# Six heads of an attention transpose by blocks and DMA instead of four, a rounding rest on another engine, and a new order of three roundings

## The chip, the cores and the metric

One core of a Trainium2 chip runs one program. The metric is the device time of that program in microseconds (us). The engines of the core are TensorE (PE in the profile, its weight loads PEld), VectorE (DVE), ScalarE (ACT), GpSimd (POOL) and SyncE (SP); each has its own stream of instructions and they meet at semaphores.

## The reference, cut to what matters

There are 128 graphs of 128 nodes with 512 features. Each graph goes through two layers.

```python
# --- layer 0: attention over the graph, 8 heads of 64 units
h = jnp.maximum(_layernorm(x), 0.0)
feats = jnp.einsum('bnf,hfu->bhnu', h, W)
dense = leaky_relu(e_self[..., :, None] + e_neigh[..., None, :], 0.2) + NEG_BIG * (1 - A)
att = softmax(dense, axis=-1)
x = x + relu(jnp.einsum('bhij,bhju->bhiu', att, feats) + b)      # heads side by side
# --- layer 1: hypergraph convolution twice, 512 -> 1024 -> 512
h = jnp.maximum(_layernorm(x), 0.0)
r = relu(Dn * H (Be * H^T (h @ W1^T)) + b1)                      # H = adj != 0
x = x + Dn * H (Be * H^T (layer_norm(r) @ W2^T)) + b2 + h        # y + x of the layer, then the residual
```

## The kernel before

The work runs in turns. In turn t the engines work on several graphs at once: the attention logits of graph t+3, the exponentials of graph t+2 (and the rest of those of t+1), the applying of the attention of t+1, the first large product (`hidden`, 512 to 1024) of graph t, the second large product (1024 to 512) of graph t-1 and the last small product of graph t-2. `turns` writes turns -5 to 1 out, loops over the middle with four turns in a loop body, and writes the last turns out. In every engine's `turn` the order of the instructions is written by hand; each engine works through its list in order, and `wait_ge` holds all that stands behind it.

The large products are made from fp32r parts: an operand is rounded by ScalarE ("hi"), the rest ("lo" = value - hi) is made by another engine, and TensorE adds hi*hi, hi*lo and lo*hi. So `hidden` needs `hg_hi` (ScalarE L572) for its first eight products and `hg_lo` (VectorE L844) for the four behind them (L890, function `low`). The second product needs `rT_hi` (ScalarE L579) and `rT_lo` (VectorE L652). The last product needs `z_hi` (ScalarE L565) and `z_lo` (GpSimd L407).

The attention weights must be transposed before they are applied. Heads 4 to 7 go through TensorE (L939), ScalarE copies them out of PSUM (L507), and they are applied at L959. Heads 0 to 3 are transposed in blocks of 32x32 by VectorE (L841, `attB`), written to HBM (L283, `att_blocks`) and read back by four DMAs (L293) that put the blocks where they belong; they are applied at L962 after a wait on `s_attD`. The exponentials come in two halves (`exps`), each head as two activations (L460, L461) whose larger one VectorE takes (`larger`, L628).

TensorE's list in one turn is: `hidden`, the last product, the four transposes, the features of chunks 0 and 1, the applying of eight heads, the second product, the features (2,0), `hg` (L992: h times G_rs, in plain fp32), the other features with the logits, and the counts p_G (L1011). VectorE's list from the end of the second product is: `z` (L792), the statistics of an x that a DMA brought (L798), the logits (L808, L818), an aggregate (L821), the transpose `eT` (L834), `attB` (L841), `hg_lo` (L844), and then the next turn's features and `rT_lo`. ScalarE's list there is: `h` (L556), `z_hi`, `hg_hi`, `rT_hi`, a copy of G. GpSimd's is: G_lo, `z_lo`, two small operations for a standard deviation (`rstd`), then a wait for the DMA that brings `u`. SP's list from eT on is: en_rows (L279), att_blocks (L283), u (L287), and the four attT transfers (L293).

Of the kernel before, what the change touches and what calls it, by code (L numbers as in the profile page):

```python
# [4 lines left out]
F32 = mybir.dt.float32  # L5
# [59 lines left out]
def gnn_two_layers(nc, x, xT, adj2, W0T, W0U, b0, a_diag, W1T, b1, gammaT, betaT, W2T, b2, out):  # L65
# [5 lines left out]
    HALF = 512  # L71
    HH = HEADS // 2
    CB = HC // 2
    UE = UN + 1
# [6 lines left out]
    with ctx:  # L81
# [55 lines left out]
        neg_max = sb("neg_max", [P, HEADS])  # L137
        attB = sb("attB", [P, HH * N])
        attT = sb("attT", [P, HEADS, N])
# [58 lines left out]

        att_blocks = nc.dram_tensor("att_blocks", [P, HH * N], F32, kind="Internal").ap()

# [28 lines left out]
        def _(sp):  # L229
# [40 lines left out]
            def turn(t):  # L270
# [18 lines left out]
                if t.plus(1).within(NG):  # L289

                    sp.wait_ge(s_attB_out, t.plus(1).count(per=16))
                    for c in range(4):
                        sp.dma_start(attT[32 * c:32 * (c + 1), 0:HH, :].rearrange("b k (q a) -> b k q a", q=4),  # L293
                                     att_blocks.rearrange("(q b) (k c a) -> c b k q a", q=4, c=4, a=32)[c]).then_inc(s_attD, 16)
# [31 lines left out]
        def _(pool):  # L326
# [19 lines left out]

            def turn(t):
                g = t.plus(2)
                if g.within(NG):
# [49 lines left out]
                if g.within(NG):  # L399
# [7 lines left out]
                    nc.gpsimd.tensor_tensor(z_lo[:, :], z[:, :], z_hi[:, :], ALU.subtract).then_inc(s_z_lo, 1)  # L407
                g = t.plus(5)
                if g.within(NG):
                    if g.has(1):  # L410
                        pool.wait_ge(s_rs0, g.count(1))
                    if g.has(4):
                        pool.wait_ge(s_feats_sb, g.count(4, per=2))
                        pool.wait_ge(s_es_low, g.count(4))
                    rstd(g, mv0, ve0, rs0[:, g.slot(4):g.slot(4) + 1], s_mv0, s_ve0, s_rs0)

# [3 lines left out]
        def _(act):  # L420
# [31 lines left out]

            def exps(g, half):

                act.wait_ge(s_shifts, g.count())
                if g.has(1):
                    act.wait_ge((s_attB, s_attT)[half], g.count(1))
                    act.wait_ge(s_att, g.count(1, per=2))
                for i in range(half * HH, (half + 1) * HH):
                    nc.scalar.activation(att[:, i, :], u[:, g.slot(2), i, :], ACT.Exp, bias=shifts[:, 0, i:i + 1])  # L460
                    last = nc.scalar.activation(att_low[:, i, :], u[:, g.slot(2), i, :], ACT.Exp, bias=shifts[:, 1, i:i + 1],  # L461
                                                scale=SLOPE)
                    if i == 2:
                        load_x(g.plus(3))
                last.then_inc(s_exp, 1)

            def turn(t):
                if t.plus(1).within(NG):

                    exps(t.plus(1), 1)  # L470
                g = t.plus(3)
# [30 lines left out]
                if g.within(NG):  # L502

                    act.wait_ge(s_attT, g.count())
                    if g.has(1):
                        act.wait_ge(s_o, g.count(1))
                    nc.scalar.activation(attT[:, HH:HEADS, :].rearrange("p h n -> p (h n)"), p_att[:, HALF:2 * HALF],  # L507
                                         ACT.Copy).then_inc(s_attT_sb, 1)
# [40 lines left out]
                if g.within(NG):  # L549

                    act.wait_ge(s_nm1, g.count())
                    if g.has(2):

                        act.wait_ge(s_hg, g.count(2))
                        act.wait_ge(s_xh, g.count(2))
                    nc.scalar.activation(h[:, g.slot(2), :], x1[:, g.slot(2), :], ACT.Relu, bias=nm1[:, :]).then_inc(s_h, 1)  # L556
                    if g.base == 0:
                        rounded(3)
                g = t.plus(-1)
                if g.within(NG):  # L560
# [4 lines left out]
                    nc.scalar.activation(z_hi[:, :], z[:, :], ACT.Copy).then_inc(s_z_hi, 1)  # L565
                g = t.plus(1)
                if g.within(NG):

                    act.wait_ge(s_hg, g.count())
                    if g.has(1):  # L570
                        act.wait_ge(s_w1, g.count(1, per=2))
                    nc.scalar.activation(hg_hi[:, :], p_w1b[:, :], ACT.Copy).then_inc(s_hg_hi, 1)  # L572
                g = t
# [26 lines left out]
        def _(dve):  # L600
# [22 lines left out]

            def larger(g, half):

                dve.wait_ge(s_exp, g.count(per=2) - 1 + half)
                heads = slice(half * HH, (half + 1) * HH)
                nc.vector.tensor_tensor(att[:, heads, :], att[:, heads, :], att_low[:, heads, :], ALU.max).then_inc(s_att, 1)  # L628
# [7 lines left out]
            def turn(t):  # L636
                g = t.plus(2)
                if g.within(NG):
# [8 lines left out]
                    feats_of(g, 1, scale)  # L647
                g = t.plus(-1)
                if g.within(NG):

                    dve.wait_ge(s_rT_hi, g.count())
                    nc.vector.tensor_tensor(rT_lo[:, :].rearrange("p (k q a) -> p k q a", q=4, a=32), rT_chunks,  # L652
                                            rT_hi[:, :].rearrange("p (k q a) -> p k q a", q=4, a=32), ALU.subtract).then_inc(s_rT_lo, 1)
                g = t
# [8 lines left out]
                if t.plus(1).within(NG):  # L663
                    larger(t.plus(1), 1)
                g = t.plus(3)
# [43 lines left out]
                if g.within(NG):  # L709
                    dve.wait_ge(s_r, g.count(per=2))  # L710
                    if g.has(1):
                        dve.wait_ge(s_rB_out, g.count(1, per=16))
                    if g.base == 0:
                        rest_of(3, k_lo2)
                        rest_of(4, k_lo2)
                        dve.wait_ge(k_lo2, 2)
                    nc.vector.transpose(rB, r[:, :]).then_inc(s_rB, 1)  # L717
# [5 lines left out]
                if g.within(NG):  # L723
# [9 lines left out]
                    if g.has(1):  # L733
                        dve.wait_ge(s_exp, g.count(1, per=2))
                    nc.vector.tensor_tensor(shifts[:, :, :], e_blk[:, SELF:SELF + EW].rearrange("p (a h) -> p a h", a=2),  # L735
# [86 lines left out]
                if m.within(NG + 2):  # L822
# [9 lines left out]
                    if g.has(2):  # L832
                        dve.wait_ge(s_exp, g.count(2, per=2))
                    nc.vector.transpose(eT[:, :], e_blk[:, :]).then_inc(s_eT, 1)  # L834
                g = t.plus(2)
                if g.within(NG):

                    dve.wait_ge(s_att, g.count(per=2) - 1)
                    if g.has(1):
                        dve.wait_ge(s_attB_out, g.count(1, per=16))  # L840
                    nc.vector.transpose(attB[:, :], att[:, 0:HH, :].rearrange("p h n -> p (h n)")).then_inc(s_attB, 1)  # L841
                if t.plus(1).within(NG):
# [6 lines left out]
        def _(pe):  # L849
# [59 lines left out]
            def transposes(dst, src, s):  # L909
                for c in range(HALF // P):  # L910
                    last = nc.tensor.transpose(dst[:, c * P:(c + 1) * P], src[:, c * P:(c + 1) * P], ident[:, :])
                last.then_inc(s, 1)

            def turn(t):
                g = t
# [17 lines left out]
                if g.within(NG):  # L933

                    pe.wait_ge(s_att, g.count(per=2))
                    if g.has(1):
                        pe.wait_ge(s_osc, g.count(1))
                    for i in range(HH, HEADS):
                        last = nc.tensor.transpose(p_att[:, i * N:(i + 1) * N], att[:, i, :], ident[:, :])  # L939
                    last.then_inc(s_attT, 1)  # L940
                g = t.plus(3)
                if g.within(NG):
# [7 lines left out]
                    for c in range(2):  # L950
                        features(c, 0)
                        features(c, 1)
                g = t.plus(1)
                if g.within(NG):

                    pe.wait_ge(s_attT_sb, g.count())
                    pe.wait_ge(s_feats_sb, g.count(per=2))
                    for i in range(HH, HEADS):
                        mm(p_o[:, i // HH, i % HH, :], attT[:, i, :], feats[:, g.slot(2), i, :], start=True, stop=True)  # L959
                    pe.wait_ge(s_attD, g.count(per=64))  # L960
                    for i in range(HH):
                        last = mm(p_o[:, 0, i, :], attT[:, i, :], feats[:, g.slot(2), i, :], start=True, stop=True)  # L962
                    last.then_inc(s_o, 1)
                if t.base == -1:
# [3 lines left out]
                if g.within(NG):  # L968

                    pe.wait_ge(s_rT_hi, g.count())  # L970
                    if t.within(NG):
                        pe.wait_ge(s_pre, t.count(per=2) - 1)
                    for c in range(HC):
                        if g.base == 0 and c % CB == 0:
                            pe.wait_ge(k_lo2, 1 + c // CB)
                        high(p_w1a[:, :], rT_hi[:, part(c)], W2_hi[:, c, :], W2_lo[:, c, :], c == 0)
                    pe.wait_ge(s_rT_lo, g.count())
                    for c in range(HC):
                        last = low(p_w1a[:, :], rT_lo[:, part(c)], W2_hi[:, c, :], c == HC - 1)
                    last.then_inc(s_w2, 1)  # L980
                g = t.plus(3)
                if g.within(NG):
                    features(2, 0)
                g = t.plus(1)
# [75 lines left out]
```

## Time and profile before

| | |
|---|---|
| median of 3 runs | 2440.66 us (2439.64 to 2444.9) |
| the profiled execution | 2446.31 us, of which the span of the trace is 2444.5 us |
| busy share of the span | PE 97%, PEld 84%, DVE 84%, ACT 70%, POOL 56% |
| HBM traffic | 166 GB/s over the span |

The span runs from the first to the last instruction. A busy TensorE need not be a fast one, since its instructions overlap; what counts is the step from one start to the next.

### The profile page before, as it was taken

The page shows a single profiled execution, that of the slowest core. Times are in us where ns is not written, and L with a number is a line of the kernel's source. Part 1 is how long each engine was busy: PE and PEld are TensorE (multiplying, and loading weights), DVE is VectorE, ACT ScalarE, POOL GpSimd, SP SyncE. Part 2 cuts the span into 40 slices and gives each one's busy share as a digit, 9 for nine tenths or more (in the row PEclk, how much of TensorE's full clock was granted, in tenths as well). Part 3 has the DMA queues.
Part 4 walks back from the last instruction along what each step waited for, and adds up shares of the span by engine and source line. Part 5 has one row for each costly group of instructions (what it writes and reads, how often), then busy time and mean ns, then how long its engine had stood idle before and what let it go on. Part 6 is the DMA issues. An engine that isn't in the chain of part 4 may idle for free.

```text
span 2444.5 us, 50002 instructions
## 1 busy us (share of the span) xinstructions
PE 2382.7 (97%) x13492; PEld 2049.6 (84%) x13492; DVE 2053.7 (84%) x4501; ACT 1713.1 (70%) x4489; POOL 1372.0 (56%) x1549
## 2 busy tenths in 40 slices
PE   5799999999999999999999999999999999999997
PEld 3688888888888888888888888888888888888886
DVE  3888888888888888888888888888888888888884
ACT  2577777777777777777777777777776777777774
POOL 2356556556556556556556556556555555555553
PEclk9799999999999999999999999999999999999999
DMA  6355555555555555555555555555555555555542
GB/s 218 104 167 170 166 171 170 167 170 169 168 171 169 167 170 170 167 170 171 168 169 169 167 170 169 167 170 170 168 169 164 172 164 170 171 167 171 172 145 86
DMA packets 494608, 405.34 MB, mean 166 GB/s; under 512 B 310648, under 2 KB 392568, under 8 KB 494584
## 3 DMA queue, kind: packets, MB, share of 16 engines
q1 hardware_dynamic: 474072, 367.30, 50.8%
q10 hardware_dynamic: 20512, 37.76, 5.5%
q8 instruction: 10, 0.16, 0.0%
q14 instruction: 14, 0.11, 0.0%
HBM read 268.58 MB, written 136.35 MB: 166 GB/s over the span
## 4 chain that ended last, share of the span: by engine, by line
PE 89%; DVE 4%; issue 2%; DMA 1%; ACT 1%; DVEq 0%; POOL 0%; POOLq 0%; ACTq 0%
PE p_w1a L885 14%; PE p_w1a L890 14%; PE p_w1a L886 14%; PE p_att L959 5%; PE p_w1b L890 5%; PE p_w1b L886 5%; PE p_w1b L885 4%; PE p_att L962 4%; PE p_w1b L992 4%; PE p_fa L881 2%; PE p_fa L879 2%; PE p_fa L880 2%; PE p_fb L880 2%; PE p_fb L881 2%; PE p_fb L879 2%; PE p_att L939 2%
## 5 line engine op out<-in xcount | busy, mean ns | idle before, releaser
L353 POOL TENSOR_TENSOR u<-u,mask 128x1024 f32<-128x1024 f32 x128 | 307.4, 2401 | 653.7 <-DMA u<-en_rows 648.4
L460 ACT ACTIVATE att<-u,shifts 128x128 f32<-128x128 f32 x1024 | 403.4, 394 | 67.1 <-DVE shifts L735 40.4
L885 PE MATMUL p_w1a<-W_hi,rT_hi 128*128 128x512 f32 x1024 | 418.0, 408 | 0.0
L886 PE MATMUL p_w1a<-W_lo,rT_hi 128*128 128x512 f32 x1024 | 406.3, 397 | 0.0
L461 ACT ACTIVATE att_low<-u,shifts 128x128 f32<-128x128 f32 x1024 | 399.0, 390 | 0.0
L407 POOL TENSOR_TENSOR z_lo<-raw,z_hi 128x512 fp32r<-128x512 f32 x128 | 165.3, 1291 | 210.7 <-ACT z_hi L565 210.7
L565 ACT ACTIVATE z_hi<-raw 128x512 fp32r<-128x512 f32 x128 | 80.9, 632 | 277.8 <-DVE raw L792 277.8
L890 PE MATMUL p_w1a<-W_hi,rT_lo 128*128 128x512 f32 x1024 | 259.8, 396 | 0.0
L890 PEld LDWEIGHTS p_w1a<-W_hi,rT_lo 128*128 128x128 f32 x1024 | 192.4, 188 | 46.6
L885 PEld LDWEIGHTS p_w1a<-W_hi,rT_hi 128*128 128x128 f32 x1024 | 194.5, 190 | 41.5 <-ACT rT_hi L579 0.7
L886 PEld LDWEIGHTS p_w1a<-W_lo,rT_hi 128*128 128x128 f32 x1024 | 194.5, 190 | 40.5
L500 ACT ACTIVATE raw<-raw 128x512 f32<-128x512 f32 x128 | 81.1, 634 | 196.5 <-DVE raw L697 196.5
L885 PE MATMUL p_w1a<-W_hi,hg_hi 128*128 128x512 f32 x512 | 213.7, 417 | 2.0 <-ACT hg_hi L572 2.0
L885 PE MATMUL p_w1b<-W_hi,hg_hi 128*128 128x512 f32 x512 | 202.6, 396 | 0.0
L886 PE MATMUL p_w1b<-W_lo,hg_hi 128*128 128x512 f32 x512 | 202.4, 395 | 0.0
L886 PE MATMUL p_w1a<-W_lo,hg_hi 128*128 128x512 f32 x512 | 202.0, 395 | 0.0
L879 PE MATMUL p_fa<-W_hi,h 128*128 128x272 f32 x512 | 170.1, 332 | 12.7 <-DVE h L669 12.7
L717 DVE STREAM_TRANSPOSE raw<-raw 128x1024 f32<-128x1024 f32 x128 | 159.5, 1246 | 22.9 <-ACT raw L500 14.3
L362 POOL TENSOR_TENSOR xc<-xT_in,u 128x512 f32<-128x512 f32 x128 | 166.2, 1298 | 20.9 <-DMA u<-en_rows 20.9
L628 DVE TENSOR_TENSOR att<-att,att_low 128x512 f32<-128x512 f32 x256 | 174.1, 680 | 3.5 <-ACT att_low L461 3.5
L377 POOL TENSOR_TENSOR raw<-x,raw 128x512 f32<-128x512 f32 x128 | 166.2, 1298 | 17.7 <-DVE shifts L735 9.9
L381 POOL TENSOR_TENSOR raw<-raw,b_bc 128x512 f32<-128x512 f32 x128 | 165.7, 1294 | 10.1
(124 smaller groups left out, 6869.6 us busy)
## 6 DMA issues: line engine op xcount, KB each, us to landing
u<-en_rows SPq DMA_DIRECT2D x130, 576.0 KB, 3.8
r_blocks<-raw SPq DMA_DIRECT2D x128, 512.0 KB, 2.6
raw<-r_blocks SPq DMA_DIRECT2D x512, 128.0 KB, 3.0
xT_in<-in_xT SPq DMA_DIRECT2D x128, 256.0 KB, 4.2
att_blocks<-attB SPq DMA_DIRECT2D x128, 256.0 KB, 2.1
attT<-att_blocks SPq DMA_DIRECT2D x512, 64.0 KB, 2.7
out<-raw SPq DMA_DIRECT2D x128, 256.0 KB, 2.0
x_in<-in_x ACTq DMA_DIRECT2D x124, 256.0 KB, 4.2
```

What stands on the lines that cost most here:

```text
L353: nc.gpsimd.tensor_tensor(u[:, g.slot(2), 0:HEADS, :], u[:, g.slot(2), 0:HEADS, :], mask[:, :].unsqueeze(1).broadcast_to([P, HEADS, N]), A ...
L362: nc.gpsimd.tensor_tensor(xc[:, :, :], xT_in[:, g.slot(2), :, :], u[:, g.slot(2), HEADS, :].unsqueeze(1).broadcast_to([P, DC, N]), ALU.sub ...
L377: nc.gpsimd.tensor_tensor(rest[s4], x1[:, s, :], rest[s4], ALU.add).then_inc(s_xh, 1)
L381: nc.gpsimd.tensor_tensor(rest[s4], rest[s4], b2_bc[:, :], ALU.add).then_inc(s_rest, 1)
L407: nc.gpsimd.tensor_tensor(z_lo[:, :], z[:, :], z_hi[:, :], ALU.subtract).then_inc(s_z_lo, 1)
L460: nc.scalar.activation(att[:, i, :], u[:, g.slot(2), i, :], ACT.Exp, bias=shifts[:, 0, i:i + 1])
L461: last = nc.scalar.activation(att_low[:, i, :], u[:, g.slot(2), i, :], ACT.Exp, bias=shifts[:, 1, i:i + 1], scale=SLOPE)
L628: nc.vector.tensor_tensor(att[:, heads, :], att[:, heads, :], att_low[:, heads, :], ALU.max).then_inc(s_att, 1)
L879: mm(dst, hi, w_hi, start=first, stop=False)
L885: mm(dst, hi, w_hi, start=first, stop=False)
L886: mm(dst, hi, w_lo, start=False, stop=False)
L890: return mm(dst, lo, w_hi, start=False, stop=final)
```

## The change

Six heads instead of four go by block transpose and DMA, two instead of four by TensorE. For this the exponentials and `larger` come in three parts: heads 0 to 3, heads 4 and 5, heads 6 and 7. The part of heads 4 and 5 stands on ScalarE behind `h`, and its `larger` on VectorE directly ahead of the `attB` transpose. On TensorE the two heads are applied behind the features (which now take (2,0) along), and the six heads behind the first chunk of the second product. `rT_lo` moves from the top of VectorE's turn to the top of GpSimd's turn, with `rstd` behind it. On ScalarE `hg_hi` comes ahead of `z_hi`.

```diff
+    HD = 6
+    PARTS = ((0, HH), (HH, HD), (HD, HEADS))
-        attB = sb("attB", [P, HH * N])
+        attB = sb("attB", [P, HD * N])
...
 # SP: the four attT transfers carry 0:HD instead of 0:HH
...
 # GpSimd, top of turn(t)
+                g = t.plus(-1)
+                if g.within(NG):
+                    pool.wait_ge(s_rT_hi, g.count())
+                    nc.gpsimd.tensor_tensor(rT_lo[:, :].rearrange("p (k q a) -> p k q a", q=4, a=32), rT_chunks,
+                                            rT_hi[:, :].rearrange("p (k q a) -> p k q a", q=4, a=32), ALU.subtract).then_inc(s_rT_lo, 1)
+                g = t.plus(4)
+                ...
+                    rstd(g, mv0, ve0, rs0[:, g.slot(4):g.slot(4) + 1], s_mv0, s_ve0, s_rs0)
 # (rstd(t+5) at the end of the turn goes)
...
 # ScalarE, turn(t)
-                    exps(t.plus(1), 1)
+                    exps(t.plus(1), 2)
...
-                    nc.scalar.activation(attT[:, HH:HEADS, :]..., p_att[:, HALF:2 * HALF], ACT.Copy)
+                    nc.scalar.activation(attT[:, HD:HEADS, :]..., p_att[:, HD * N:HEADS * N], ACT.Copy)
...
                     nc.scalar.activation(h[:, g.slot(2), :], x1[:, g.slot(2), :], ACT.Relu, bias=nm1[:, :]).then_inc(s_h, 1)
+                if t.plus(2).within(NG):
+                    exps(t.plus(2), 1)
+                # hg_hi of t+1 here, ahead of z_hi of t-1
...
 # VectorE, turn(t)
-                    nc.vector.tensor_tensor(rT_lo[:, :]..., rT_chunks, rT_hi[:, :]..., ALU.subtract).then_inc(s_rT_lo, 1)
...
                     nc.vector.transpose(eT[:, :], e_blk[:, :]).then_inc(s_eT, 1)
                 g = t.plus(2)
                 if g.within(NG):
-                    dve.wait_ge(s_att, g.count(per=2) - 1)
+                    larger(g, 1)
+                    dve.wait_ge(s_att, g.count(per=3) - 1)
-                    nc.vector.transpose(attB[:, :], att[:, 0:HH, :].rearrange("p h n -> p (h n)")).then_inc(s_attB, 1)
+                    nc.vector.transpose(attB[:, :], att[:, 0:HD, :].rearrange("p h n -> p (h n)")).then_inc(s_attB, 1)
...
 # TensorE
+            def apply_rest(g):
+                pe.wait_ge(s_attD, g.count(per=64))
+                for i in range(HD):
+                    last = mm(p_o[:, i // HH, i % HH, :], attT[:, i, :], feats[:, g.slot(2), i, :], start=True, stop=True)
+                last.then_inc(s_o, 1)
 # transposes and the applying behind the features: range(HD, HEADS) instead of range(HH, HEADS)
                         features(c, 0)
                         features(c, 1)
+                    features(2, 0)
...
+                    high(p_w1a[:, :], rT_hi[:, part(0)], W2_hi[:, 0, :], W2_lo[:, 0, :], True)
+                if t.plus(1).within(NG):
+                    apply_rest(t.plus(1))
+                if g.within(NG):
+                    for c in range(1, HC):
+                        high(p_w1a[:, :], rT_hi[:, part(c)], W2_hi[:, c, :], W2_lo[:, c, :], False)
                     pe.wait_ge(s_rT_lo, g.count())
                     ...
-                    features(2, 0)
```

## Rows read from the trace of the kernel before

**Rows 1.** Windows view: stretch, length, busy PE, PEld, DVE, ACT, POOL, clock, DMA share, GB/s.
```profile
200.00:2300.00 2100.00, 2097.14 (x12014) 1811.67 (x12013) 1813.40 (x4002) 1520.87 (x4006) 1222.39 (x1373) 1.00 0.58 169
```

**Rows 2.** View by line of L844, 220 to 2300 us: durations, first and last start.
```profile
L844 DVE TENSOR_TENSOR hg_lo<-p_w1b,hg_hi x113: 649/652/655, 231.3 to 2287.8; 128x512 fp32r<-128x512 f32 x113
```

**Rows 3.** Timeline of PE: start, length (us), line, operation, count.
```profile
1211.81 0.47 PE L885 MATMUL p_w1a<-W_hi,rT_hi 128*128 128x512 f32 x1
...
1217.48 0.29 PE L879 MATMUL p_fa<-W_hi,h 128*128 128x272 f32 x1
...
1217.86 1.05 PE L992 MATMUL p_w1b<-G_rs,h 128*128 128x128 f32 x8
...
1219.97 0.48 PE L885 MATMUL p_w1a<-W_hi,hg_hi 128*128 128x512 f32 x1
...
1221.91 1.10 PE L890 MATMUL p_w1a<-W_hi,hg_lo 128*128 128x512 f32 x4
...
1226.35 0.60 PE L939 MATMUL p_att<-ident,att 128*128 128x128 f32 x4
1226.71 0.37 PE L879 MATMUL p_fa<-W_hi,h 128*128 128x272 f32 x1
...
1230.05 0.48 PE L885 MATMUL p_w1a<-W_hi,rT_hi 128*128 128x512 f32 x1
1230.36 0.39 PE L886 MATMUL p_w1a<-W_lo,rT_hi 128*128 128x512 f32 x1
```

**Rows 4.** Timeline of DVE in the same turn.
```profile
1218.35 0.68 DVE L798 BATCH_NORM_STATS2 st<-x_in 128x6 f32<-128x512 f32 x1
1219.32 0.24 DVE L808 TENSOR_SCALAR e_blk<-p_fa,rs 128x16 f32<-128x16 f32 x1 [0.29 <-PE p_fa L881]
...
1220.15 0.21 DVE L834 STREAM_TRANSPOSE eT<-e_blk 128x32 f32<-128x32 f32 x1 [0.32 <-DVE e_blk L821]
1220.29 0.68 DVE L841 STREAM_TRANSPOSE attB<-att 128x512 f32<-128x512 f32 x1
1220.90 0.65 DVE L844 TENSOR_TENSOR hg_lo<-p_w1b,hg_hi 128x512 fp32r<-128x512 f32 x1
```

**Rows 5.** Timelines of DVE and PE in a turn whose hg_lo was late.
```profile
1331.48 0.65 DVE L844 TENSOR_TENSOR hg_lo<-p_w1b,hg_hi 128x512 fp32r<-128x512 f32 x1
...
1332.19 1.20 PE L890 MATMUL p_w1a<-W_hi,hg_lo 128*128 128x512 f32 x4 [0.22 <-DVE hg_lo L844]
```

**Rows 6.** View by line and form: instructions, busy us, mean ns of one, idle before.
```profile
L628 DVE TENSOR_TENSOR att<-att,att_low 128x512 f32<-128x512 f32 x256 | 174.1, 680 | 3.5 <-ACT att_low L461 3.5
...
L717 DVE STREAM_TRANSPOSE raw<-raw 128x1024 f32<-128x1024 f32 x128 | 159.5, 1246 | 22.9 <-ACT raw L500 14.3
```

**Rows 7.** L763 of DVE by its view (ns min/median/max) and timelines beside a POOL operation.
```profile
L763 DVE SCALAR_TENSOR_TENSOR inv<-G,inv x129: 152/328/593, 44.9 to 2408.4; 128x2 f32<-128x2 f32 x129
...
1213.92 1.29 POOL L381 TENSOR_TENSOR raw<-raw,b_bc 128x512 f32<-128x512 f32 x1
...
1214.90 0.33 DVE L763 SCALAR_TENSOR_TENSOR inv<-G,inv 128x2 f32<-128x2 f32 x1
```

**Rows 8.** Timelines of ACT and POOL in the turn of rows 3.
```profile
1218.46 0.63 ACT L565 ACTIVATE z_hi<-raw 128x512 fp32r<-128x512 f32 x1 [2.13 <-DVE raw L792]
1219.00 0.58 ACT L572 ACTIVATE hg_hi<-p_w1b 128x512 fp32r<-128x512 f32 x1
1219.48 1.05 ACT L579 ACTIVATE rT_hi<-raw 128x1024 fp32r<-128x1024 f32 x1
...
1219.17 1.29 POOL L407 TENSOR_TENSOR z_lo<-raw,z_hi 128x512 fp32r<-128x512 f32 x1 [1.57 <-ACT z_hi L565]
```

**Rows 9.** Waits view: waiter, releaser, total us, times, longest us.
```profile
DVE st L798 <- DMA x_in<-in_x: 23.0, 49, 1.1
```

**Rows 10.** Timeline of SP's four attT transfers; DMA view's KB and us to landing.
```profile
1204.96 2.64 SPq L293 DMA_DIRECT2D attT<-att_blocks  x4
...
attT<-att_blocks SPq DMA_DIRECT2D x512, 64.0 KB, 2.7
```

More of the change, by code:

```diff
@@ L197, in gnn_two_layers @@
         r_blocks = nc.dram_tensor("r_blocks", [P, DH], F32, kind="Internal").ap()
-        att_blocks = nc.dram_tensor("att_blocks", [P, HH * N], F32, kind="Internal").ap()
+        att_blocks = nc.dram_tensor("att_blocks", [P, HD * N], F32, kind="Internal").ap()
         block = ctx.enter_context(nc.Block())
@@ L292, in turn @@
                     for c in range(4):
-                        sp.dma_start(attT[32 * c:32 * (c + 1), 0:HH, :].rearrange("b k (q a) -> b k q a", q=4),
+                        sp.dma_start(attT[32 * c:32 * (c + 1), 0:HD, :].rearrange("b k (q a) -> b k q a", q=4),
                                      att_blocks.rearrange("(q b) (k c a) -> c b k q a", q=4, c=4, a=32)[c]).then_inc(s_attD, 16)
@@ L347, in turn @@
             def turn(t):
+                g = t.plus(-1)
[5 more added lines that the diff above has]
+                if g.within(NG):
+                    if g.has(1):
+                        pool.wait_ge(s_rs0, g.count(1))
+                    if g.has(4):
+                        pool.wait_ge(s_feats_sb, g.count(4, per=2))
+                        pool.wait_ge(s_es_low, g.count(4))
+                    rstd(g, mv0, ve0, rs0[:, g.slot(4):g.slot(4) + 1], s_mv0, s_ve0, s_rs0)
                 g = t.plus(2)
@@ L407, in turn @@
                     nc.gpsimd.tensor_tensor(z_lo[:, :], z[:, :], z_hi[:, :], ALU.subtract).then_inc(s_z_lo, 1)
[L408 to L415, printed above, removed]
             turns(pool, turn, NG)
@@ L451, in load_x, with exps @@
                     act.dma_start(x_in[:, g.slot(4), :], x[bass.ds(n, 1), :, :].rearrange("a p d -> p (a d)")).then_inc(s_in[g.slot(4)], 16)
-            def exps(g, half):
+            def exps(g, part):
                 act.wait_ge(s_shifts, g.count())
                 if g.has(1):
-                    act.wait_ge((s_attB, s_attT)[half], g.count(1))
-                    act.wait_ge(s_att, g.count(1, per=2))
-                for i in range(half * HH, (half + 1) * HH):
+                    act.wait_ge((s_attB, s_attB, s_attT)[part], g.count(1))
+                    act.wait_ge(s_att, g.count(1, per=3))
+                for i in range(*PARTS[part]):
                     nc.scalar.activation(att[:, i, :], u[:, g.slot(2), i, :], ACT.Exp, bias=shifts[:, 0, i:i + 1])
@@ L506, in turn @@
                         act.wait_ge(s_o, g.count(1))
-                    nc.scalar.activation(attT[:, HH:HEADS, :].rearrange("p h n -> p (h n)"), p_att[:, HALF:2 * HALF],
+                    nc.scalar.activation(attT[:, HD:HEADS, :].rearrange("p h n -> p (h n)"), p_att[:, HD * N:HEADS * N],
                                          ACT.Copy).then_inc(s_attT_sb, 1)
@@ L558, in turn @@
                         rounded(3)
+                if t.plus(2).within(NG):
+                    exps(t.plus(2), 1)
+                g = t.plus(1)
+                if g.within(NG):
+                    act.wait_ge(s_hg, g.count())
+                    if g.has(1):
+                        act.wait_ge(s_w1, g.count(1, per=2))
+                    nc.scalar.activation(hg_hi[:, :], p_w1b[:, :], ACT.Copy).then_inc(s_hg_hi, 1)
                 g = t.plus(-1)
@@ L565, in turn @@
                     nc.scalar.activation(z_hi[:, :], z[:, :], ACT.Copy).then_inc(s_z_hi, 1)
[L566 to L572, printed above, removed]
                 g = t
@@ L622, in centre, with larger @@
                 last.then_inc(k_cent, 1)
-            def larger(g, half):
-                dve.wait_ge(s_exp, g.count(per=2) - 1 + half)
-                heads = slice(half * HH, (half + 1) * HH)
+            def larger(g, part):
+                dve.wait_ge(s_exp, g.count(per=3) - 2 + part)
+                heads = slice(*PARTS[part])
                 nc.vector.tensor_tensor(att[:, heads, :], att[:, heads, :], att_low[:, heads, :], ALU.max).then_inc(s_att, 1)
@@ L647, in turn @@
                     feats_of(g, 1, scale)
[L648 to L653, printed above, removed]
                 g = t
@@ L663, in turn @@
                 if t.plus(1).within(NG):
-                    larger(t.plus(1), 1)
+                    larger(t.plus(1), 2)
                 g = t.plus(3)
@@ L711, in turn @@
                     if g.has(1):
+                        dve.wait_ge(s_rT_lo, g.count(1))
                         dve.wait_ge(s_rB_out, g.count(1, per=16))
@@ L733, in turn @@
                     if g.has(1):
-                        dve.wait_ge(s_exp, g.count(1, per=2))
+                        dve.wait_ge(s_exp, g.count(1, per=3))
                     nc.vector.tensor_tensor(shifts[:, :, :], e_blk[:, SELF:SELF + EW].rearrange("p (a h) -> p a h", a=2),
@@ L832, in turn @@
                     if g.has(2):
-                        dve.wait_ge(s_exp, g.count(2, per=2))
+                        dve.wait_ge(s_exp, g.count(2, per=3))
                     nc.vector.transpose(eT[:, :], e_blk[:, :]).then_inc(s_eT, 1)
@@ L933, in turn @@
                 if g.within(NG):
-                    pe.wait_ge(s_att, g.count(per=2))
+                    pe.wait_ge(s_att, g.count(per=3))
                     if g.has(1):
                         pe.wait_ge(s_osc, g.count(1))
-                    for i in range(HH, HEADS):
+                    for i in range(HD, HEADS):
                         last = nc.tensor.transpose(p_att[:, i * N:(i + 1) * N], att[:, i, :], ident[:, :])
@@ L957, in turn @@
                     pe.wait_ge(s_feats_sb, g.count(per=2))
-                    for i in range(HH, HEADS):
+                    for i in range(HD, HEADS):
                         mm(p_o[:, i // HH, i % HH, :], attT[:, i, :], feats[:, g.slot(2), i, :], start=True, stop=True)
[L960 to L963, printed above, removed]
                 if t.base == -1:
@@ L972, in turn @@
                         pe.wait_ge(s_pre, t.count(per=2) - 1)
[L973 to L976, printed above, removed]
+                    if g.base == 0:
+                        pe.wait_ge(k_lo2, 2)
+                    high(p_w1a[:, :], rT_hi[:, part(0)], W2_hi[:, 0, :], W2_lo[:, 0, :], True)
+                if t.plus(1).within(NG):
+                    apply_rest(t.plus(1))
+                if g.within(NG):
+                    for c in range(1, HC):
+                        high(p_w1a[:, :], rT_hi[:, part(c)], W2_hi[:, c, :], W2_lo[:, c, :], False)
                     pe.wait_ge(s_rT_lo, g.count())
@@ L980, in turn @@
                     last.then_inc(s_w2, 1)
-                g = t.plus(3)
-                if g.within(NG):
-                    features(2, 0)
                 g = t.plus(1)
```

## The prediction

> **What bounds the kernel now.** I read the windows first: in the steady stretch TensorE is busy 2097 of 2100 us at a granted clock of 1.00, the full 2.4 GHz level, and no other engine is [rows 1]. So the length is the sum of TensorE's turns, and a gain must shorten TensorE's list. The mean turn is (2287.8 - 231.3) / 112 = 18.36 us, from the first and the last of 113 starts of one instruction that runs once a turn [rows 2]. The TensorE timeline then gives one turn in steps: from one start of the second product to the next, 1230.05 - 1211.81 = 18.24 us [rows 3]; the other 0.12 us of the mean are small waits.
>
> A busy engine can still have a neighbour that is only just in time, so I next read what arrives last. The point is `hg_lo`. In rows 3 and 4 the second product ends at 1217.48 (the next instruction starts there); I call this time 0 of the turn. VectorE makes hg_lo from 3.42 to 4.07, and TensorE starts the four products that need it at 4.43. That is 0.36 us of margin, and part of it isn't margin at all: in a turn where hg_lo was late, its end at 1332.13 let TensorE start at 1332.19, and the group lasted 1.20 instead of 1.10 us, so that an hg_lo which sets the time counts 0.06 + 0.10 = 0.16 us after its end [rows 3 to 5]. True margin in this turn: 0.20 us. The reader is to see that VectorE's list between time 0 and hg_lo is a second path, almost as long as TensorE's own, though VectorE is busy only 86% of the stretch [rows 1].
>
> **The change part by part, on TensorE.** Two transposes go. Four take 1226.71 - 1226.35 = 0.36 us, so two save 0.18. The applying of the attention is now cut in two by two fp32r products. Going from plain fp32 back to fp32r costs time: the first step of the second product is 0.31 us [rows 3], while the eight products of `hidden` take 1.94 us in steps of (1.94 - 0.31) / 7 = 0.23, so each such return costs 0.08, and there is one more. The features (2,0) only move. Sum: 18.24 - 0.18 + 0.08 = 18.14 us for a turn without any wait.
>
> Moving (2,0) has a second effect. It took 1217.86 - 1217.48 = 0.38 us between time 0 and hg [rows 3]. Without it TensorE wants hg_lo at 4.43 - 0.38 = 4.05 instead of 4.43.
>
> **On VectorE.** rT_lo leaves a place behind hg_lo, so it doesn't help hg_lo. Ahead of hg_lo come two costs. `larger` over 256 columns: 512 cost 0.680; the rest of that fits 1.07 ns a column (attB's 0.68 to 0.70 for 512 and 1.246 for 1024 columns give 0.55 / 512), so 0.41 us, and 0.03 until attB, which needs its result, can start [rows 4, 6]. The transpose of 768 columns instead of 512 adds 0.27, and its step becomes 0.61 + 0.27 = 0.88 us. One thing comes sooner: the logits follow hg and come at 1219.32 - 1217.48 - 0.38 = 1.46; the statistics ahead of them, started at 0.87 with about 0.6 us to the next instruction, allow the same [rows 4]. From the logits to eT are 0.83, from eT to the next instruction 0.14. So `larger` is ready to start at 1.46 + 0.83 + 0.14 = 2.43. If nothing held it, hg_lo would start at 2.43 + 0.44 + 0.88 = 3.75, end at 4.40, and count at 4.56: 0.51 us after TensorE wants it.
>
> **What holds it.** `larger` reads two SBUF tensors. The trace shows such an instruction being held by GpSimd: L763 does two columns, takes 0.152 us at its shortest and 0.328 at the median; in the rows beside it, it starts in the middle of a GpSimd addition and ends at 1215.23, just behind the end of that addition at 1215.21 [rows 7]. So it did its 0.15 us of work from about 0.13 before that end. The Trainium skill has the rule, in "SBUF — State Buffer", section "SBUF: two separate sides": VectorE with two SBUF inputs and GpSimd take turns on a shared port pair, as an exclusive lock for a whole instruction. It speaks against moving work to GpSimd; the row agrees that one waits for the other, but sets the release 0.13 us earlier. By the rule to the letter my time below would be 0.13 us a turn longer, some 16 us.
>
> Where is GpSimd at 2.43? hg takes 1.05 us [rows 3] and now starts at 0, so hg_hi can start at about 1.09; z_hi behind it steps 0.48 (as rT_hi does behind hg_hi now), runs 0.63 and ends at 2.20; z_lo follows 0.08 later, from 2.28 to 3.57 [rows 8]. Before, z_hi came first and z_lo ran from 1.69 to 2.98, beside nothing with two SBUF inputs. Now z_lo has started 0.15 us before `larger` can. So `larger` ends at 3.57 - 0.13 + 0.41 = 3.85, hg_lo starts at 3.85 + 0.03 + 0.88 = 4.76, ends at 5.41 and counts at 5.57. TensorE stands still for 5.57 - 4.05 = 1.52 us in each turn.
>
> **The rest of the change** I cost at nothing. The two heads of exponentials behind `h` are four activations that left the top of ScalarE's turn; they fit in the 2.13 us that ScalarE stood idle before z_hi [rows 8]; without that cover they would push hg_hi. rT_lo on GpSimd takes about 2 x 1.29 = 2.6 us, by z_lo with half the columns [rows 8], in a stretch where GpSimd waits for the u transfer; TensorE wants it only behind the hi products of the next second product. `rstd` moves behind it and is wanted a turn later. SP holds u's transfer behind the wait for attB. attB ended at 3.49 and will end at 3.88 + 0.97 = 4.85, 1.36 later, but TensorE's own list is 5.57 - 4.43 = 1.14 later too, so 0.2 us is left; VectorE transposes r meanwhile, so this is covered, and costs 0.2 if not.
>
> The six heads' transfers: the four issues began at 1204.96 and took 2.64, so the last began near 1206.9 and landed 2.7 later, at 1209.6 [rows 10]; the last four heads were applied ahead of 1211.81 in about 1 us, by hg's like products [rows 3]. Margin 1.2 us, and by the same counting it stays so. Half as much again costs nothing at the least, and at the most half of each: 1.3 for a write as long as the read, 1.0 for the issues, 1.3 for the landing, together 3.6. The four landings overlap, issued 0.66 apart and each 2.7 long, so most of the 2.7 is not moving bytes; I take a third, 1.2. So no wait, but a bound of 2.4 us.
>
> **Sum.** 18.14 + 1.52 = 19.66 us a turn, against 18.36: 1.30 more. Over some 122 turns in their full form, 159 us. The profiled execution took 2446.3 us, 5.6 above the median of the runs, so it would take 2605, and the median **2599 us**. Its own bounds: z_lo 0.3 us sooner, 2562, to the port held to z_lo's end and z_lo 0.2 us later, 2639.
>
> **The rivals.**
> - *Unheld.* If `larger` takes the port before z_lo, the stall is 0.51 us and the turn 18.65: 0.29 x 122 = 35 us, 2476. The waits for x_in that eT absorbs now (23.0 us in all, 0.18 a turn [rows 9]) then show: up to 2498. For it: only 0.15 us decide. Against: any lateness of x puts `larger` behind z_lo's start.
> - *GpSimd goes on.* When z_lo ends, rT_lo is ready behind it. If GpSimd takes the port again before VectorE, `larger` waits 2.6 us more: 2599 + 317 = 2916. No row has a waiting VectorE and two GpSimd operations back to back. Against: in rows 7 the release comes before the end.
> - *Transfers late.* If the six heads cost 2.4 us and not 1.2, half way to their bound, TensorE waits 1.2 us more ahead of them: 2599 + 146 = 2745. For it: the margin is worked out to be nothing. Against: the overlap of the landings.
> - *Faster.* If VectorE's path to hg_lo stayed under 3.9 us, the turn would be 18.14: 0.22 x 122 = 27 us gained, 2414. It decides at 0.5 us less than the unheld path that I work out, and the rows show no part of it that large that could vanish.
>
> **How the numbers follow.** Held, as forecast: 0.58. Unheld: 0.18. GpSimd goes on: 0.08. Transfers late: 0.08. Faster 0.04, and no change beyond 0.2% (about what a measurement can tell) 0.04, if the parts happen to cancel. Median 2599; the range takes in the held and the unheld case and part of the late transfers: 2470 to 2660. Slower 0.92, same 0.04, faster 0.04.
>
> **What would show it.** In the profile after: a TensorE wait for hg_lo at L890 in nearly every turn, some 1.5 us (0.5 if unheld, 4 if GpSimd goes on); the new 256-column `larger` recorded with 1.4 us rather than 0.4, ending with z_lo; rT_lo on GpSimd near 2.6 us without a waiter; no wait for attD. The forecast falls if `larger` starts ahead of z_lo, or if hg_lo ends before 4 us after the second product.

## The result and the profile after

The changed kernel takes 2588.0 us at the median (2584.1 to 2590.3), against 2442.8 us before; the ratio is 1.0579 with a 95% interval of 1.056 to 1.0598. The forecast was 2599 us. The profiled execution has a span of 2586.2 us. One run among those below, of the kernel with r's rest back on VectorE, lay 2.1% above the fastest of its kernel, and its median leaves that run out.

The windows view of the changed kernel over the same stretch as [rows 1] (stretch, length, busy PE, PEld, DVE, ACT, POOL, clock, DMA share, GB/s), and the view by line of hg_lo, as [rows 2]:

```profile
200.00:2300.00 2100.00, 1954.84 (x11074) 1666.33 (x11075) 1729.34 (x3762) 1399.11 (x3759) 1416.91 (x1398) 1.00 0.59 172
...
L851 DVE TENSOR_TENSOR hg_lo<-p_w1b,hg_hi x106: 651/652/653, 238.8 to 2290.7; 128x512 fp32r<-128x512 f32 x106
```

TensorE is no longer busy all the time: 145 of 2100 us are idle, at a clock that is still 1.00. The mean turn is (2290.7 - 238.8) / 105 = 19.54 us instead of 18.36; 1.18 us more, over some 124 turns, is the whole difference.

The waits view says what the idle time ended on (waiter, releaser, total us, times, longest us):

```profile
PE p_w1a L897 <- DVE hg_lo L851: 162.3, 120, 1.4
...
PEld p_att L925 <- DMA attT<-att_blocks: 2.1, 5, 1.2
```

So TensorE waits for hg_lo, in 120 turns, 1.35 us each, and hardly for the six heads' transfers (2.1 us in all). Why hg_lo is late is in the timelines of one turn. First PE:

```profile
1203.64 0.55 PE L974 MATMUL p_att<-feats,attT 128*128 128x65 f32 x4
1204.01 0.48 PE L892 MATMUL p_w1a<-W_hi,rT_hi 128*128 128x512 f32 x1
...
1204.55 1.45 PE L925 MATMUL p_att<-feats,attT 128*128 128x65 f32 x12
1205.81 0.48 PE L892 MATMUL p_w1a<-W_hi,rT_hi 128*128 128x512 f32 x1
...
1211.01 1.05 PE L1004 MATMUL p_w1b<-G_rs,h 128*128 128x128 f32 x8
...
1213.13 0.47 PE L892 MATMUL p_w1a<-W_hi,hg_hi 128*128 128x512 f32 x1
...
1216.52 1.20 PE L897 MATMUL p_w1a<-W_hi,hg_lo 128*128 128x512 f32 x4 [1.29 <-DVE hg_lo L851]
...
1221.06 0.38 PE L953 MATMUL p_att<-ident,att 128*128 128x128 f32 x2
1221.19 0.37 PE L886 MATMUL p_fa<-W_hi,h 128*128 128x272 f32 x1
```

Then DVE:

```profile
1211.21 0.75 DVE L798 SCALAR_TENSOR_TENSOR raw<-p_w1a,rs,t_bc 128x512 f32<-128x512 f32 x1 [0.44 <-PE p_w1a L897]
...
1212.48 0.23 DVE L814 TENSOR_SCALAR e_blk<-p_fa,rs 128x16 f32<-128x16 f32 x1
...
1213.32 0.21 DVE L840 STREAM_TRANSPOSE eT<-e_blk 128x32 f32<-128x32 f32 x1 [0.32 <-DVE e_blk L827]
1213.45 1.43 DVE L639 TENSOR_TENSOR att<-att,att_low 128x256 f32<-128x256 f32 x1
1214.91 0.98 DVE L848 STREAM_TRANSPOSE attB<-att 128x768 f32<-128x768 f32 x1
1215.81 0.65 DVE L851 TENSOR_TENSOR hg_lo<-p_w1b,hg_hi 128x512 fp32r<-128x512 f32 x1
```

And ACT and POOL:

```profile
1212.10 0.60 ACT L576 ACTIVATE hg_hi<-p_w1b 128x512 fp32r<-128x512 f32 x1 [1.10 <-PE p_w1b L1004]
1212.60 0.62 ACT L583 ACTIVATE z_hi<-raw 128x512 fp32r<-128x512 f32 x1
...
1213.30 1.30 POOL L423 TENSOR_TENSOR z_lo<-raw,z_hi 128x512 fp32r<-128x512 f32 x1 [2.20 <-ACT z_hi L583]
1214.56 2.55 POOL L354 TENSOR_TENSOR rT_lo<-raw,rT_hi 128x1024 fp32r<-128x1024 f32 x1
```

The second product ends at 1211.01. The reader is to see one row: `larger` on 256 columns is recorded with 1.43 us. It starts 0.15 us after z_lo and ends at 1214.88, 0.28 us after z_lo's end. The same operation on the 256 columns of heads 6 and 7, at 1218.60, takes 0.42 us. From there attB and hg_lo follow without a gap, and TensorE, ready at 1213.13 + 1.94 = 1215.07, starts at 1216.52, 1.45 us late; the view counts 1.29 of it as idle, from the end that it gives the product before.

This turn is like nearly all. In 119 of the 124 turns in which `larger` and z_lo overlap, `larger` is recorded with more than 1 us, and in the median it ends 0.28 us after z_lo's end. Four turns, near the start and the end of the run, went the other way: there `larger` started first, took its 0.38 us, and z_lo was recorded longer, up to 1.51 us. DVE and POOL in one of them:

```profile
2483.39 0.38 DVE L639 TENSOR_TENSOR att<-att,att_low 128x256 f32<-128x256 f32 x1
...
2483.42 1.51 POOL L423 TENSOR_TENSOR z_lo<-raw,z_hi 128x512 fp32r<-128x512 f32 x1 [2.25 <-ACT z_hi L583]
```

So the later of the two waited, whichever it was.

### The profile page after: what moved, and what is told of

The parts are those of the page before. It is cut to its first block and busy times, and to the rows that moved or that the text cites. A ratio compares the mean times of both kernels' runs of the same rounds, so it can differ in the third digit from the quotient of the medians.

```text
span 2586.2 us, 50225 instructions
## 1 busy us (share of the span) xinstructions
PE 2362.2 (91%) x13236; PEld 2005.1 (78%) x13236; DVE 2073.9 (80%) x4501; ACT 1680.3 (65%) x4489; POOL 1693.1 (65%) x1677
## 5 line engine op out<-in xcount | busy, mean ns | idle before, releaser
L892 PE MATMUL p_w1a<-W_hi,rT_hi 128*128 128x512 f32 x1024 | 426.7, 417 | 0.7 <-ACT rT_hi L590 0.7
L354 POOL TENSOR_TENSOR rT_lo<-raw,rT_hi 128x1024 fp32r<-128x1024 f32 x128 | 324.8, 2537 | 5.8 <-ACT rT_hi L590 5.7
L639 DVE TENSOR_TENSOR att<-att,att_low 128x256 f32<-128x256 f32 (+1 forms) x384 | 299.9, 781 | 2.6 <-ACT att_low L469 2.6
L897 PE MATMUL p_w1a<-W_hi,hg_lo 128*128 128x512 f32 x512 | 152.9, 420 | 162.4 <-DVE hg_lo L851 162.3
L490 ACT ACTIVATE raw<-raw 128x512 f32<-128x512 f32 x128 | 81.1, 633 | 328.1 <-DVE raw L666 328.1
L897 PEld LDWEIGHTS p_w1a<-W_hi,hg_lo 128*128 128x128 f32 x512 | 86.5, 188 | 228.3 <-DVE hg_lo L851 216.6
L508 ACT ACTIVATE raw<-raw 128x512 f32<-128x512 f32 x128 | 81.0, 633 | 189.3 <-DVE raw L702 189.3
L925 PEld LDWEIGHTS p_att<-feats,attT 128*128 128x128 f32 x1536 | 190.5, 191 | 13.0 <-DMA attT<-att_blocks 2.1
```

Of the source, the lines that this page charges most:

```text
L354: nc.gpsimd.tensor_tensor(rT_lo[:, :].rearrange("p (k q a) -> p k q a", q=4, a=32), rT_chunks, rT_hi[:, :].rearrange("p (k q a) -> p k q a ...
L490: nc.scalar.activation(r[:, 0:HALF], r[:, 0:HALF], ACT.Relu, accum_out=sum2[:, 0:1]).then_inc(s_r, 1)
L892: mm(dst, hi, w_hi, start=first, stop=False)
L897: return mm(dst, lo, w_hi, start=False, stop=final)
L925: last = mm(p_o[:, i // HH, i % HH, :], attT[:, i, :], feats[:, g.slot(2), i, :], start=True, stop=True)
```

## The experiments

Three explanations were on trial. The theory: GpSimd's z_lo holds VectorE's `larger`, and hg_lo behind it is late. Rival 1: VectorE's list ahead of hg_lo is simply longer. Rival 2: the rest of r's transpose on GpSimd costs. Each kernel is the changed one with the edit shown, shortened where `...` or a comment stands for lines. Times are medians; each ratio is to the kernel before as it was timed beside that run (medians from 2444 to 2454 us), with its 95% interval.

**z_lo after the larger.**

```diff
                     pool.wait_ge(s_z_hi, g.count())
+                    if t.plus(2).within(NG):
+                        pool.wait_ge(s_att, t.plus(2).count(per=3) - 1)
                     nc.gpsimd.tensor_tensor(z_lo[:, :], z[:, :], z_hi[:, :], ALU.subtract).then_inc(s_z_lo, 1)
```

> GpSimd waits with z_lo until VectorE has taken the larger of heads 4 and 5. Theory (the larger is held by z_lo): it starts 2.4 us after the second product and takes 0.4 us instead of 1.2 to 1.4, hg_lo comes about 1 us sooner, TensorE's wait for hg_lo falls from 1.3 to about 0.4 us a turn, and the time from 2588 to 2465 to 2495 us. Rival 1 (VectorE's list ahead of hg_lo is simply longer, whatever GpSimd does): 2580 to 2595. Rival 2 (the rest of r's transpose on GpSimd is what costs): no gain either, 2580 or more, since that operation only comes later.

Measured: 2471.9 us, 1.0107 times before (1.0077 to 1.0137): 116 of the 145 us come back by a wait on GpSimd. The timelines of DVE, POOL and PE, where the second product ends at 1212.08:

```profile
1214.53 0.40 DVE L641 TENSOR_TENSOR att<-att,att_low 128x256 f32<-128x256 f32 x1
...
1215.00 1.30 POOL L425 TENSOR_TENSOR z_lo<-raw,z_hi 128x512 fp32r<-128x512 f32 x1 [2.89 <-DVE att L641]
...
1212.08 1.05 PE L1006 MATMUL p_w1b<-G_rs,h 128*128 128x128 f32 x8
...
1216.65 1.20 PE L899 MATMUL p_w1a<-W_hi,hg_lo 128*128 128x512 f32 x4 [0.35 <-DVE hg_lo L853]
```

`larger` starts at the same 2.45 us after the second product and takes 0.40. This settles the theory against rival 1 for the larger part of the loss. What is left of the wait, 0.35 us idle in this turn and 50.1 us in all, is what the longer list leaves when nothing is held.

**z rounded ahead of hg.** The two blocks of ScalarE change places.

```diff
-                # hg_hi of t+1, then z_hi of t-1
+                # z_hi of t-1, then hg_hi of t+1
```

> ScalarE rounds z ahead of hg again, all else as after the change. Theory: z_lo ends 0.6 us sooner, and with it the larger of heads 4 and 5 and hg_lo; hidden starts up to 0.1 us later; the turn falls by about 0.6 us and the time to 2500 to 2525. Rival 1 and rival 2: no gain, 2580 to 2600, or a small loss since hidden starts later.

Measured: 2516.6 us, ratio 1.0287 (1.0258 to 1.0316). The timelines of DVE, POOL and PE:

```profile
1216.56 0.60 DVE L639 TENSOR_TENSOR att<-att,att_low 128x256 f32<-128x256 f32 x1
...
1215.59 1.29 POOL L423 TENSOR_TENSOR z_lo<-raw,z_hi 128x512 fp32r<-128x512 f32 x1 [1.61 <-ACT z_hi L576]
...
1213.89 1.05 PE L1004 MATMUL p_w1b<-G_rs,h 128*128 128x128 f32 x8
...
1218.89 1.19 PE L897 MATMUL p_w1a<-W_hi,hg_lo 128*128 128x512 f32 x4 [0.72 <-DVE hg_lo L851]
```

z_lo runs from 1.70 to 2.99 us after the second product instead of 2.29 to 3.59, and `larger` ends 0.28 us after it again, at 3.27. The end of `larger` moves with the end of z_lo, by 0.60 us. So one edit of the change, the order of these two roundings (hg ahead of z), costs 71 us with the others in place.

**r's rest back on VectorE.**

```diff
-                    nc.gpsimd.tensor_tensor(rT_lo..., rT_chunks, rT_hi..., ALU.subtract).then_inc(s_rT_lo, 1)
+                    # the same on VectorE, behind feats_of(g, 1, scale)
```

> The rest of r's transpose is made on VectorE again, behind the features. Theory: z_lo holds the larger of heads 4 and 5 as before, so hg_lo comes no sooner: 2575 to 2600. Rival 2 (the move to GpSimd costs): most of the 146 us come back, 2450 to 2500.

Measured: 2747.9 us, ratio 1.1255 (1.1207 to 1.1303). Both missed: it is 160 us slower still. TensorE's wait for hg_lo is what it was (162.4 us in all), so rival 2 falls, but there is a new loss. The view by line of a two-column count, and the timelines of DVE, POOL and PE in a turn that is longer:

```profile
L696 DVE TENSOR_SCALAR cnt<-G x129: 161/170/2405, 37.1 to 2684.8; 128x2 f32<-128x2 f32 x129
...
1231.04 2.40 DVE L696 TENSOR_SCALAR cnt<-G 128x2 f32<-128x2 f32 x1
...
1231.04 2.38 POOL L363 TENSOR_TENSOR u<-u,mask 128x1024 f32<-128x1024 f32 x1 [5.05 <-DMA u<-en_rows]
...
1235.41 0.66 PE L974 MATMUL p_att<-feats,attT 128*128 128x65 f32 x4 [1.61 <-ACT attT L509]
```

With 1.2 us more on its list VectorE comes to that count just as GpSimd begins the mask addition, and two columns take 2.40 us, as long as that addition. This happens in 55 of 129 counts and adds 121 us to them. What stands behind the count is late too: the second half of r, ScalarE's copy of the attention, and TensorE, which waits 89.0 us in all for that copy. TensorE's granted clock was 0.97 between 1100 and 1300 us, where the changed kernel has 1.00; how the 160 us divide between the waits and the clock was not separated.

**The mask addition after the counts**, in that last kernel, to test this reading.

```diff
                     pool.wait_ge(s_mask, g.count())
+                    pool.wait_ge(s_inv0, g.count())
```

> The kernel with r's rest back on VectorE, and GpSimd's mask addition waits until VectorE has made its small counts. Theory (there the mask addition held a two-column count for 2.4 us, since r's rest had pushed VectorE's list into it): the count takes 0.2 us in every turn and the time falls to 2580 to 2630. Rival (VectorE's list is simply too long with r's rest on it): 2700 or more.

Measured: 2585.9 us, ratio 1.0551 (1.0526 to 1.0576), and no count above 0.171 us. The whole extra loss is gone, and r's rest costs nothing on VectorE as long as z_lo sets the time.

**hg_lo ahead of the larger and attB.**

```diff
+                # hg_lo here, right behind eT
                     larger(g, 1)
                     ...
                     nc.vector.transpose(attB[:, :], att[:, 0:HD, :]...).then_inc(s_attB, 1)
-                # hg_lo here
```

> VectorE makes hg_lo right behind eT, and the larger of heads 4 and 5 and their transpose after it. Theory: the wait for hg_lo goes (it ends about 3.1 us after the second product, wanted at 4.0); the larger is still held until z_lo ends, attB ends at about 4.9 as now, and TensorE, now 1.5 us sooner at the six heads, waits there about 0.7 us for their transfers: 2480 to 2515. Rival 1 (nothing is held): attB ends 0.4 us sooner, a wait of 0.3 us, 2430 to 2465.

Measured: 2526.5 us, ratio 1.0331 (1.0298 to 1.0364), 11 us above the theory's range. The wait for hg_lo is gone; the waits view shows what came in its place:

```profile
PE p_att L925 <- DMA attT<-att_blocks: 96.7, 127, 2.6
...
DVE neg_max L732 <- POOL u L369: 129.3, 127, 2.7
```

TensorE waits 0.76 us a turn for the six heads, where 0.7 was worked out. Not foreseen was the second row: u's transfer stands behind the wait for attB on SP, and VectorE now waits 1.0 us a turn for it. Such a wait need not cost time: the fastest kernel below has 84.2 us of it. Where the extra 11 us come from stays open.

**Four heads again**, with the other edits of the change.

```diff
-    HD = 6
-    PARTS = ((0, HH), (HH, HD), (HD, HEADS))
+    HD = HH
+    PARTS = ((0, HH), (HH, HEADS))
     # and no exps / larger of a middle part
```

> The change without its six heads: four heads by blocks and four by TensorE again, two parts of exponentials; the move of r's rest to GpSimd, the order of the roundings and TensorE's new order stay. Theory: no larger stands between eT and attB, so nothing is held; hg_lo ends 3.7 us after the second product and TensorE wants it at 4.0; the turn is 18.1 to 18.3 us, 2405 to 2440. Rival 2 (the move to GpSimd costs): 2500 or more. Rival 1 (length of VectorE's list): as the theory.

Measured: 2421.6 us, ratio 0.9881 (0.9839 to 0.9924). Without the two heads the rest of the change is a gain of 1.2%. z_lo is as late as in the changed kernel (it starts 1205.51 - 1203.22 = 2.29 us after the second product), but no operation on VectorE stands beside it that it is seen to hold.

**The larger early.** It goes between z and the statistics, and hg_lo goes ahead of attB.

```diff
                     nc.vector.scalar_tensor_tensor(z[:, :], p_w1a[:, :], ...).then_inc(s_z, 1)
+                if t.plus(2).within(NG):
+                    larger(t.plus(2), 1)
                 ...
                     nc.vector.transpose(eT[:, :], e_blk[:, :]).then_inc(s_eT, 1)
+                # hg_lo here
-                    larger(g, 1)
                     # attB
```

> All of the change, but VectorE takes the larger of heads 4 and 5 right behind z, ahead of the statistics, where GpSimd runs nothing, and makes hg_lo ahead of attB. Theory: no operation is held (0.41 us for that larger), the wait for hg_lo goes, attB ends 4.3 us after the second product and the six heads land about 0.2 us late: a turn of 18.2 us, 2415 to 2455. Rival 1 (the longer list alone): the same list lies ahead of attB, so a wait of 0.5 us or more moves to the transfers, 2465 to 2500.

Measured: 2425.7 us, ratio 0.9893 (0.9851 to 0.9935). All six heads, and 162 us faster than the change as it was made. Two edits were made at once here, so this run does not say what each is worth.

**The six heads applied one chunk later**, on top of that.

```diff
                     high(p_w1a[:, :], rT_hi[:, part(0)], W2_hi[:, 0, :], W2_lo[:, 0, :], True)
+                    high(p_w1a[:, :], rT_hi[:, part(1)], W2_hi[:, 1, :], W2_lo[:, 1, :], False)
                 if t.plus(1).within(NG):
                     apply_rest(t.plus(1))
                 if g.within(NG):
-                    for c in range(1, HC):
+                    for c in range(2, HC):
```

> As the kernel with the larger early, and TensorE applies the six heads one chunk of the second product later (0.47 us). If the six heads' transfers are what is left of the waits, this covers them: a turn of 18.0 us, 2390 to 2425. If the end of the applying is what the rest of the turn hangs on (h and G_rs for hg), the time is that of the kernel with the larger early or up to 30 us longer.

Measured: 2396.9 us, ratio 0.9780 (0.9739 to 0.982). This beats both kernels. What the weight loads of the six heads' products waited for their transfers, first with the larger early, then here, shows that the first of the two readings holds:

```profile
PEld p_att L926 <- DMA attT<-att_blocks: 51.3, 124, 0.8
...
PEld p_att L926 <- DMA attT<-att_blocks: 8.8, 24, 1.0
```

Its view by line of hg_lo, and the timelines of DVE, POOL and PE:

```profile
L845 DVE TENSOR_TENSOR hg_lo<-p_w1b,hg_hi x116: 647/649/653, 227.6 to 2292.4; 128x512 fp32r<-128x512 f32 x116
...
1212.74 0.41 DVE L639 TENSOR_TENSOR att<-att,att_low 128x256 f32<-128x256 f32 x1
...
1214.57 0.65 DVE L845 TENSOR_TENSOR hg_lo<-p_w1b,hg_hi 128x512 fp32r<-128x512 f32 x1
...
1214.16 1.30 POOL L423 TENSOR_TENSOR z_lo<-raw,z_hi 128x512 fp32r<-128x512 f32 x1 [1.87 <-ACT z_hi L583]
1215.42 2.40 POOL L354 TENSOR_TENSOR rT_lo<-raw,rT_hi 128x1024 fp32r<-128x1024 f32 x1
...
1215.93 1.10 PE L898 MATMUL p_w1a<-W_hi,hg_lo 128*128 128x512 f32 x4
```

`larger` is through 1.0 us before z_lo starts, hg_lo ends at 1215.22 and TensorE takes it at 1215.93 without a wait. The turn is (2292.4 - 227.6) / 115 = 17.95 us.

**That kernel with r's rest on VectorE**, by the edit shown above for it.

> The fastest kernel so far (larger early, six heads applied later), with r's rest on VectorE again. It prices that move where nothing is held. Theory: VectorE's list gets 1.2 us longer between the features and the first half of r, but ends ahead of the mask addition; 2395 to 2430. If the list runs into the mask addition, some turns lose 1 to 2 us and the time is 2450 to 2550. Rival 2 (the move to GpSimd costs): below 2390.

Measured: 2418.5 us, ratio 0.9867 (0.9839 to 0.9894). No count is held here (none above 0.172 us), so this prices the move of r's rest to GpSimd where nothing is held: it is worth 22 us, and rival 2 is wrong in sign. Where the 22 us arise was not followed.

## Why the prediction was right

**Direction and size.** The forecast hung on one chain, and each of its links was found where it was put, in us after the end of the second product: z_lo's start 2.28 forecast, 2.29 measured; `larger` ready 2.43 and 2.44; its end 3.85 and 3.87; hg_lo's start 4.76 and 4.80. That it is a hold and not a longer list is shown by the two kernels that move z_lo: the end of `larger` follows the end of z_lo, and without z_lo beside it, it takes 0.40 us.

**The unheld rival** is what ran where z_lo was made to wait: 2471.9 us, 4 below the 2476 to 2498 worked out, and a wait for hg_lo of 50 us in all instead of 162. In the changed kernel itself it came in the four turns above. The forecast gave the hold 0.15 us to decide by; in the median of the 124 turns `larger` starts 0.23 us after z_lo.

**GpSimd goes on** did not happen. In the changed kernel rT_lo stands ready behind z_lo, yet `larger` ends 0.28 us after z_lo. rT_lo takes 2.55 us there and 2.40 in the fastest kernel, where no VectorE operation waits; that fits VectorE going first and GpSimd waiting some 0.15 us, but no view shows this wait by itself.

**The terms that were mis-sized.** TensorE's turn without a wait was 18.14 in the sum and is some 17.95. Two terms were too dear. Two transposes take 1221.19 - 1221.06 = 0.13 us, so the step saves 0.23 and not 0.18. And the applying of eight heads, left at its old length of about 1.78 us in my sum, takes 0.37 + 1.26 = 1.63 us in two groups; why the groups are faster was not tested. The extra return to fp32r is there, 0.31 instead of 0.23 us at each of the two places, as counted. The stall was 1.52 in the sum and is 19.54 - 17.95 = 1.59, if the fastest kernel's turn is taken for the one without a wait; in the rows above it is 1.45 and 1.20 - 1.10 = 0.10 for the longer group, 1.55. The errors of the turn and of the stall have opposite signs, so that the total lies nearer than TensorE's own term is partly luck: the turn came to 19.66 forecast and 19.54 measured, and with it 2599 against 2588 us.

**The transfers** were priced too high. The DMA view and SP's timeline of the changed kernel, beside [rows 10]:

```profile
att_blocks<-attB SPq DMA_DIRECT2D x128, 384.0 KB, 2.5
attT<-att_blocks SPq DMA_DIRECT2D x512, 96.0 KB, 2.7
...
1218.49 2.73 SPq L295 DMA_DIRECT2D attT<-att_blocks  x4
```

The read-back lands after 2.7 us as before, the four issues take 2.73 instead of 2.64, and the write lands after 2.5 us; it had 2.1 in the profile before. That is 0.5 us, where I took 1.2. The rival of late transfers had no ground in this kernel; such a wait did show, at 0.76 us a turn, in the kernel with hg_lo ahead, where hg_lo no longer kept TensorE back.

**Cost at nothing.** The exponentials behind `h` and the copy by ScalarE cost nothing that a view shows: hg_hi starts 1212.10 - 1211.01 = 1.09 us after the second product, as in the sum. u's transfer was covered, as I took it to be: VectorE waits 5.7 us for it in all. The move of r's rest to GpSimd, which I also put at nothing, costs nothing in the changed kernel (2588.0 us with it, 2585.9 without it and with the counts kept clear). What my sum did not look for is the other side: in this order the same work on VectorE pushes the counts into the mask addition.

## What to carry to other kernels

Before moving work between VectorE and GpSimd, lay their timelines side by side and mark, on VectorE, every operation with two SBUF inputs, and tensor-scalars from SBUF to SBUF such as the count: a start some 0.2 us on the wrong side of a GpSimd operation cost about 1 us a turn here, and a short operation pays for what is left of the long one. An operation recorded far longer than its shape needs, whose end follows the end of something on the other engine, is that sign. When an input of the engine that sets the time comes only just in time, what is put ahead of it beyond its margin is paid in full, so put it behind; the same six heads went from 5.8% slower to 2.2% faster by where the pieces stand.

## What the runs showed of the hardware that was not expected

A hold also strikes an operation with one SBUF tensor: the two-column count above is a tensor-scalar that reads one, and took 2.40 us instead of 0.17. The trace of the kernel before had this already, in one turn of the steady stretch, where it could have been seen. DVE and POOL there:

```profile
1849.13 2.40 DVE L691 TENSOR_SCALAR cnt<-G 128x2 f32<-128x2 f32 x1
...
1849.12 2.39 POOL L353 TENSOR_TENSOR u<-u,mask 128x1024 f32<-128x1024 f32 x1 [4.74 <-DMA u<-en_rows]
```

The Trainium skill, "SBUF — State Buffer", section "SBUF: two separate sides", names VectorE's 2-port modes beside two inputs, and its part "Who interferes with whom" has tensor-scalars among the operations that can enter them. The held count fits that; which mode it ran in, no run shows.

Not every GpSimd operation holds for its recorded time. The timelines of POOL and DVE in the changed kernel:

```profile
1204.85 0.55 POOL L386 TENSOR_TENSOR rs<-ve,halfpow 128x1 f32<-128x1 f32 x1
...
1205.01 0.17 DVE L734 TENSOR_TENSOR neg_s<-neg_max,e_blk 128x8 f32<-128x8 f32 x1
1205.21 0.17 DVE L736 SCALAR_TENSOR_TENSOR neg_m<-neg_s 128x8 f32<-128x8 f32 x1
```

Both VectorE operations take two SBUF inputs (the second takes neg_s twice), lie inside a GpSimd power of one column, and run at their usual 0.17 us. So it is in all 191 places of this trace where a small VectorE operation of this group lies inside such a power: none is longer than 0.17 us. A one-column operation's 0.55 us hold next to nothing.

For long operations the rows say less. `larger`, worth 0.41 us, ends 0.28 us behind z_lo's end. Either the hold ends about 0.13 us before the recorded end, as the prediction has it, or the first 0.13 us of `larger` need nothing that z_lo holds; the times come out the same, and no run tells the two apart. The Trainium skill, in the same section, has the shared ports locked for the whole instruction. The long operations agree with that to within these 0.13 us; the one-column power does not.
